# A SwiGLU block's gate/up weight slabs: 1024 rows in one buffer in place of 512 rows in two

## What is computed

```
def ternary_matmul(x, w):
    return jnp.matmul(x, jnp.sign(w).T)
xq = activation_quant(rms_norm(x))
g = jax.nn.silu(ternary_matmul(xq, W_g))
u = ternary_matmul(xq, W_u)
p = g * u
return ternary_matmul(p, W_d)
```

## Time and profile before

| | us |
|---|---|
| median of 2 runs | 6451.73 |
| the two runs | 6428.04, 6475.41 |
| profiled execution, time | 6456.98 |
| profiled execution, span of the slowest core (core 0) | 6455.4 |
| spans of the 8 cores | 6380.9 to 6455.4 |
| TensorE busy (share of the span) | 2955.8 (46%) |
| ACT busy | 1533.4 (24%) |
| DVE busy | 1137.4 (18%) |

### The profile page before, as it was taken

How to read it: one execution, slowest core, us unless ns; L and a number is a source line. 1 busy time by engine, 2 the same in 40 slices (tenths; PEclk the granted TensorE clock), 3 DMA queues, 4 the chain that set the end, 5 groups by cost and what they waited for, 6 DMA issues and landing times.

```text
span 6455.4 us, 38883 instructions; the slowest of 8 cores (6380.9 to 6455.4 us)
## 1 busy us (share of the span) xinstructions
PE 2955.8 (46%) x11876; PEld 1162.8 (18%) x12108; DVE 1137.4 (18%) x2467; ACT 1533.4 (24%) x1600; POOL 379.6 (6%) x725
## 2 busy tenths in 40 slices
PE   2444441443344723444336006677343367884443
PEld 1222210110011300111012002233121123331121
DVE  0111211332233212333223430000000000000000
ACT  2444322443344223444333430000000000000000
POOL 1000020000001310000011000000000000000000
PEclk9666665776777856777768557888677687776667
DMA  6555174223324553322332014444322244443222
GB/s 131 124 123 124 46 125 97 49 55 67 69 54 72 83 105 72 61 49 57 71 73 44 0 65 99 99 99 100 89 61 67 67 99 100 99 99 86 61 60 61
DMA packets 998483, 510.30 MB, mean 79 GB/s; under 512 B 853892, under 2 KB 890760, under 8 KB 991112
## 3 DMA queue, kind: packets, MB, share of 16 engines
q1 hardware_dynamic: 842504, 251.86, 16.7%
q0 software_dynamic: 100480, 155.23, 16.5%
q10 hardware_dynamic: 55296, 100.69, 4.2%
HBM read 327.16 MB, written 117.44 MB: 69 GB/s over the span
## 4 chain that ended last, share of the span: by engine, by line
SPq 30%; DMA 22%; PE 19%; ACT 14%; issue 7%; DVE 6%; POOL 1%; ACTq 1%; DVEq 0%; POOLq 0%; another core or an unknown queue 0%
SPq L946 10%; SPq L956 10%; PE psw L1056 7%; SPq L1029 5%; SPq L1039 5%; DMA pin<-wg 5%; DMA pin<-wu 5%; ACT expw L721 5%; DMA pin<-wd 4%; ACT pin L252 3%; PE psw L366 3%; DMA scrg<-pin 2%; DMA scru<-pin 2%; DMA scrd<-pin 2%; DVE expw L739 2%
## 5 line engine op out<-in xcount | busy, mean ns | idle before, releaser
L972 PE MATMUL psw<-xqT,wg 128*128 128x512 bf16 x2007 | 563.8, 441 | 432.2 <-DMA wu<-scru 429.0
L252 ACT ACTIVATE pin<-pin 128x1024 bf16<-128x1024 bf16 x384 | 405.2, 1055 | 1382.2 <-DMA pin<-wg 506.3
L704 PE MATMUL psw<-qT,kT 128*128 128x512 bf16 x494 | 196.5, 398 | 1107.5 <-ACT expw L721 1000.7
L721 ACT ACTIVATE expw<-psw,smalls 128x1024 bf16<-128x1024 f32 x512 | 570.5, 1114 | 467.4 <-PE psw L707 459.1
L1056 PE MATMUL psw<-wd3k,pT 128*128 128x512 bf16 x1005 | 250.0, 409 | 682.2 <-DMA wd3v<-scrd 680.8
L989 ACT ACTIVATE gs<-psw 128x512 f32<-128x512 f32 x128 | 76.4, 597 | 1927.5 <-PE psf L977 1927.5
L977 PE MATMUL psf<-xqT,wu 128*128 128x512 bf16 x2007 | 495.2, 400 | 2.7
L739 DVE TENSOR_TENSOR expw<-expw,maskb 128x512 bf16<-128x512 bf16 x512 | 217.7, 425 | 1342.9 <-ACT expw L721 1342.9
L972 PEld LDWEIGHTS psw<-xqT,wg 128*128 128x128 bf16 x2048 | 222.8, 110 | 757.7 <-issue 638.5
L997 DVE TENSOR_TENSOR pT<-gs,psf 128x512 bf16<-128x512 f32 x128 | 88.0, 688 | 1371.6 <-ACT gs L989 1371.6
L341 PE MATMUL pstr<-identT,h1b 128*128 128x128 bf16 x640 | 81.0, 303 | 514.7 <-ACT h1b L322 504.0
(11 more groups left out here) (118 smaller groups left out, 2642.3 us busy)
## 6 DMA issues: line engine op xcount, KB each, us to landing
xst<-x_full SPq DMA_DIRECT2D x32, 1024.0 KB, 5.0
pin<-wg POOLq DMA_DIRECT2D x128, 256.0 KB, 4.9
scrg<-pin ACTq DMA_DIRECT2D x128, 256.0 KB, 2.3
pin<-wu POOLq DMA_DIRECT2D x128, 256.0 KB, 4.9
scru<-pin ACTq DMA_DIRECT2D x128, 256.0 KB, 2.1
pin<-wd POOLq DMA_DIRECT2D x128, 256.0 KB, 4.7
scrd<-pin ACTq DMA_DIRECT2D x128, 256.0 KB, 2.2
wpr<-wq POOLq DMA_DIRECT2D x128, 128.0 KB, 6.8
```

Of the source, the lines that this page charges most:

```text
L252: c.activation(tile, tile, AF.Sign).then_inc(cS.h, 1)
L704: t.matmul(psw[:, 0:512], kT[:, kv * S + sb * 128:kv * S + (sb + 1) * 128], qT3[:, h0, :], start=True, stop=True)
L721: c.activation(expw[sb % 2][:, :], psw[:, :], AF.Exp, bias=sml[:, 106:107]).then_inc(cS.h, 1)
L972: ins = t.matmul(psf[pbg][:, :], wg3[:, wsl, c_, hsub * 128:(hsub + 1) * 128], xqT3[:, c_, pss * 512:(pss + 1) * 512], start=(c_ == 0), st ...
```

## The change

wg3 and wu3 keep their size and place, but each becomes one buffer of 1024 columns: [128, 16, 1024] in place of [128, 2, 16, 512]. The loop over 16 slabs of 512 rows becomes a loop over 8 slabs of 1024 rows (`pr2`). Each of its 32 transposing DMAs now reads 1024 rows by 128 columns and writes a [128, 1024] piece, so a pass issues 256 of them where it issued 512. SP waits once a slab, and for the matmuls of the slab before it (`wfree` is a single number); the wait ahead of the wu transposes goes. The two semaphores dTR[0] and dTR[1] still alternate. TensorE runs eight groups a slab instead of four; the order of the matmuls, activations and multiplications is the same. The down part is not changed.

```
--- before.py
+++ after.py
@@ -86,10 +86,10 @@
         resid = at("resid", [128, 16384], F32, RA)
         pT = at("pT", [128, 32768], BF16, RA)
         kT = at("kT", [128, 16384], BF16, RBK)
-        wg3 = at("wg3", [128, 2, 16, 512], BF16, RBK)
+        wg3 = at("wg3", [128, 16, 1024], BF16, RBK)
         wd3k = at("wd3k", [128, 32, 512], BF16, RBK)
         vtm = at("vtm", [128, 16384], BF16, RBV)
-        wu3 = at("wu3", [128, 2, 16, 512], BF16, RBV)
+        wu3 = at("wu3", [128, 16, 1024], BF16, RBV)
         wd3v = at("wd3v", [128, 32, 512], BF16, RBV)
         wkv = at("wkv", [128, 16384], BF16, RC)
         wpr3 = at("wpr3", [128, 2, 16, 512], BF16, RC)
@@ -934,48 +934,43 @@
                     name=nc.get_next_instruction_name(), act_func_set_id=18, ins=[], outs=[]))
 
             for pss in range(2):
-                wfree = [0, 0]
+                wfree = 0
                 gsfree = [0, 0]
-                for hs in range(16):
-                    wsl = hs % 2
+                for pr2 in range(8):
+                    par2 = pr2 % 2
 
                     @em("sync")
-                    def _(s, hs=hs, wsl=wsl, wf=wfree[wsl]):
+                    def _(s, pr2=pr2, par2=par2, wf=wfree):
                         s.wait_ge(tS.h, wf)
                         for c_ in range(16):
                             s.dma_start_transpose(
-                                wg3[:, wsl, c_, :],
-                                scrg[hs * 512:(hs + 1) * 512,
-                                     c_ * 128:(c_ + 1) * 128]).then_inc(dTR[wsl].h, 16)
-                    dTR[wsl].n += 256
-
-                    @em("sync")
-                    def _(s, hs=hs, wsl=wsl, wf=wfree[wsl]):
-                        s.wait_ge(tS.h, wf)
+                                wg3[:, c_, :],
+                                scrg[pr2 * 1024:(pr2 + 1) * 1024,
+                                     c_ * 128:(c_ + 1) * 128]).then_inc(dTR[par2].h, 16)
                         for c_ in range(16):
                             s.dma_start_transpose(
-                                wu3[:, wsl, c_, :],
-                                scru[hs * 512:(hs + 1) * 512,
-                                     c_ * 128:(c_ + 1) * 128]).then_inc(dTR[wsl].h, 16)
-                    dTR[wsl].n += 256
-                    wrdy = dTR[wsl].n
-                    for hsub in range(4):
+                                wu3[:, c_, :],
+                                scru[pr2 * 1024:(pr2 + 1) * 1024,
+                                     c_ * 128:(c_ + 1) * 128]).then_inc(dTR[par2].h, 16)
+                    dTR[par2].n += 512
+                    wrdy = dTR[par2].n
+                    for hsub in range(8):
                         pbg = hsub % 2
                         pbu = 2 + hsub % 2
 
                         @em("tensor")
-                        def _(t, pss=pss, wsl=wsl, hsub=hsub, pbg=pbg, pbu=pbu, wrdy=wrdy,
+                        def _(t, pss=pss, par2=par2, hsub=hsub, pbg=pbg, pbu=pbu, wrdy=wrdy,
                               pfg=psfree[pbg], pfu=psfree[pbu]):
-                            t.wait_ge(dTR[wsl].h, wrdy)
+                            t.wait_ge(dTR[par2].h, wrdy)
                             t.wait_ge(vS.h, max(pfg, pfu))
                             for c_ in range(16):
                                 ins = t.matmul(psf[pbg][:, :],
-                                               wg3[:, wsl, c_, hsub * 128:(hsub + 1) * 128],
+                                               wg3[:, c_, hsub * 128:(hsub + 1) * 128],
                                                xqT3[:, c_, pss * 512:(pss + 1) * 512],
                                                start=(c_ == 0), stop=(c_ == 15))
                             for c_ in range(16):
                                 ins = t.matmul(psf[pbu][:, :],
-                                               wu3[:, wsl, c_, hsub * 128:(hsub + 1) * 128],
+                                               wu3[:, c_, hsub * 128:(hsub + 1) * 128],
                                                xqT3[:, c_, pss * 512:(pss + 1) * 512],
                                                start=(c_ == 0), stop=(c_ == 15))
                             ins.then_inc(tS.h, 1)
@@ -991,9 +986,9 @@
                         slv = cS.n
 
                         @em("vector")
-                        def _(v, pss=pss, hs=hs, hsub=hsub, pbu=pbu, slv=slv, gsl=hsub % 2):
+                        def _(v, pss=pss, pr2=pr2, hsub=hsub, pbu=pbu, slv=slv, gsl=hsub % 2):
                             v.wait_ge(cS.h, slv)
-                            slot = hs * 4 + hsub
+                            slot = pr2 * 8 + hsub
                             v.tensor_tensor(pT[:, slot * 512:(slot + 1) * 512],
                                             gsb[gsl], psf[pbu][:, :],
                                             ALU.mult).then_inc(vS.h, 1)
@@ -1001,7 +996,7 @@
                         psfree[pbg] = vS.n
                         psfree[pbu] = vS.n
                         gsfree[hsub % 2] = vS.n
-                    wfree[wsl] = tS.n
+                    wfree = tS.n
                 pT_done = vS.n
                 if "d_pT" in dbg and pss == 0:
                     @em("sync")
```

## The result

| | before | after |
|---|---|---|
| median of the runs, us | 6455.74 (10 runs) | 6785.18 (11 runs) |
| ratio of comparable runs, with 95% interval | 1 | 1.045 [1.0404, 1.0496] |
| profiled execution, us | 6456.98 | 6695.81 |

The change makes the kernel 4.5% slower, where about 11% had been forecast; in the profiled executions it is 238.8 us. In five of the 11 runs after, cores of one die or both show a lower granted clock and take longer; the ratio leaves these out, the median does not.

What follows compares the result with a forecast made beforehand. SP's DMA issue was taken to bound gate/up. Per 1024 rows, 71.7 us issue, 61.9 landing and matmuls and 0.6 later landing make 134.2; sixteen make 2147 against 1430, +717, so 7170 us, range 6900 to 7420.

Steps and rivals of the forecast that it cites:

- What bounds the kernel before: Gate/up stage of both passes: goes at SP's issue pace, 1.30 us a transpose, with TensorE's work inside it; 1429.8 us together.
- The overlap is lost: Gate/up with one buffer: issue and matmuls no longer overlap; SP's 32 transposes wait for the previous slab's last matmul.
- the model: Down stage's serial load-then-matmul cycle, taken as pattern for gate/up: 145.3 us mean, of which 83.4 us is issue.
- The price of a 1024-row transpose: SP's issue in gate/up: a fixed part plus a part per row, 2.24 us from one wide transpose to the next.
- What remains after the issue: Gate/up, each 1024 rows: 61.9 us for last landing and matmuls from the down-stage cycle, plus 0.6 us later landing.
- my mean: Down-stage cycles of both passes averaged, 142.5 and 148.1 us to 145.3, including pass 1's slower matmuls.
- Rival 2: Gate/up issue: flat cost per transpose whatever its rows, 1.30 us; stage +237 us, kernel 6690 us; chance 0.10.
- My own lower bound for the transfer: DMA engines in gate/up: a wide transpose needs about 1.27 us, from 0.63 us for one of 512 rows.
- the DMA share of 31%: Sign named for the gate/up stage: the DMA engines' busy share must fall from 46% to about 31%.
- Rival 3: Gate/up: wide transposes go at the speed bytes move, 376 GB/s, 0.70 us each; -73 us, kernel 6380 us; chance 0.04.
- 6690 and 7355: Kernel times in us for two gate/up issue prices: flat per transpose, chance 0.10, and wholly per row, chance 0.30.

Runs made afterwards that it cites:

- the narrow run with the new order: Changed kernel with all eight gate groups before all eight up groups and each 1024-row transpose split into two of 512; 6445 us, ratio 0.9994 to the kernel before.
- The narrow run with one buffer: Changed kernel with each 1024-row transpose made two of 512, single buffer kept; 7323 us, ratio 1.1329 to the kernel before.

## Why the prediction was right and wrong

- What bounds the kernel before: right. SP's issue did, as the row without a hole said; the narrow run with the new order, which changes the order of the groups and the use of the buffers but not the number of issues, has the same time.
- The overlap is lost, and the down stage is the model for it: right. The narrow run with one buffer takes 143.3 us for 1024 rows against 145.3 in the model; the stage came to 1146.8 us a pass where 8 x 145.3 = 1162 was worked out.
- The price of a 1024-row transpose: this is the step that failed. I took p = 2.24 us, 328 ns fixed and 934 ns that go with the rows. The measured pace is 45.3/32 = 1.41 us, and 1.26 to 1.31 us from 64 to 768 rows. The difference of 0.83 us by 512 transposes is 423 us, another 16 x 1.7 = 27 are in the next point, and the forecast lay 717 - 267.6 = 449 above the stage's loss. The argument compared two kinds of instruction, a plain copy and a transpose, and read the difference between them as a slope over packets; all the transposes in the trace had one size, so there was no slope to read. The wide transposes did have twice the packets, 1056 against 544, and SP's median issue went from 1262 to 1300 ns; the rest, up to 1.41 us, comes with engines that are full.
- What remains after the issue: 62.5 us forecast, 106.1 - 45.3 = 60.8 measured. The landing grew more than the 0.6 us I gave it, from 2.7 to 4.2, and the matmuls were 57.8 us in the slab shown; pass 1 ran at the same pace as pass 0 here, where my mean held slower matmuls of before. Those belonged to cores and not to the kernel: from 5138 to 5855 of that same execution, pass 1's gate/up, TensorE was busy 538 to 552 us on cores 0, 1, 6 and 7, at a granted clock of 0.75 to 0.77, and 478 to 482 us on cores 2 to 5, at 0.83.
- Rival 2, the flat price with 0.10 of the chance, is what happened: a price for each instruction and not for each row. It gave +237 us for the stage, which lost 267.6: 1.41 for 1.30 us costs 57 more, 60.8 for 62.5 gives 27 back. That the profiled executions differ by 238.8 in all is luck: the down parts gave 10 back and the stage began 18.7 earlier, on another core. Its sentence that the engines would have no reserve was no argument against it but a correct forecast, 0.94 busy. My own lower bound for the transfer, 1.27 us, fell short of the 1.41 us at which the engines then held the pace: it took a wide transpose for twice a narrow one, 325 us of engine time a pass, and it was 385. That, and a stage shorter than forecast, is why the DMA share of 31% that I named as a sign did not come.
- Rival 3, bytes at 376 GB/s: wrong, the burst moved 173 GB/s with full engines. The Trainium skill's 350 to 400 GB/s for transposing DMAs (Advanced Engine Details and Errata, X-Bar Transpose (TRN2)) is not met here at any size: 182 GB/s at 2048 rows with the engines full, at most 198, at 4096 rows. Its other rule, to merge small transfers (DMA: Bandwidth & Descriptors, Rules for kernel authors), which I weighed as nearly worthless above 64 KB, held further than that mark: from 128 to 256 KB the issue of a slab fell from 83.4 to 45.3 us. Above 256 KB merging brought nothing more, 2.76 us for 2048 rows.
- The range of 6900 to 7420 left rival 2 out. Between ends as far apart as 6690 and 7355, with nothing but an analogy between them, it should have held the lower one.

The timed runs show more than the profile, 4.5% against 3.7%. That goes with the clock: over 56 pairs of core and execution of the changed kernel (the six runs in the ratio and the profiled one), the span falls by 45 us for each 0.01 of mean granted clock (least squares; core 0 for instance has 6674.7 us at 0.726 and 6754.8 at 0.711), over 152 pairs of the kernel before by 25 us. A likely reading is that TensorE was beside SP's issue and is now in line with it, so whatever slows it is paid in full. It is not shown: this is an association over executions, and no run here sets the clock.

## What to carry to other kernels

Ask of a merged transfer which price it divides: here the issue price of a transpose is per instruction, so merging halves it until the engines are full, but the time is only won if something still runs beside it. Before a buffer is given up for larger pieces, look for an order in which two operands' buffers take turns: gate then up gave the overlap back with the same weight memory, and 18% came from doing so in both stages with wide pieces. And a price for a size that no row shows should be bounded by its extremes until a probe with several sizes in one kernel has measured it.

## What the runs showed of the hardware

- A DMA transpose of 128 columns costs SP 1.26 to 1.31 us of issue from 64 to 768 rows, nearly four times a plain 1 MB copy's 0.33 us. What in the instruction takes that time is open: no run here changed the number of columns, and none issued transposes from another engine than SP.
- From 1024 rows on, the 16 engines are the limit, at 0.92 to 1.02 busy and 167 to 198 GB/s; plain loads in the trace of before reached 376 GB/s in a slice. For the same 71.4 MB the engines are busy 385 us with 1024 rows and 325 with 512; why is open.
- TensorE kept a granted clock of 0.97 over 1380 us at 95% busy. The interrupted stages had 0.69 to 0.82. In the changed kernel's first burst, with TensorE idle, the granted clock is 0.50 (1.2 GHz), and it is still 0.50 from 3882 to 3886, over the first matmuls after the wait; from 3888 to 3940 it is 1.00. The first group of 16 takes 5.97 us, the later ones 3.62.
- A third value stands in the trace of the kernel before: from 6100 to 6140, with TensorE busy 39.7 of 40 us, the granted clock is 0.81, and 32 matmuls take 8.58 us instead of 7.07. What brings it is open.
